# Inputs laid out transposed outside the program, layer-norm folds moved from VectorE to TensorE, x loaded on two queues

## Chip, cores and metric

The kernel runs on one core of a Trainium2 chip. The metric is the device time of one execution in microseconds (us). TensorE is called PE, VectorE DVE, ScalarE ACT, GpSimd POOL and SyncE SP; PEld is TensorE's loading of weights. One program holds five instruction streams that meet at semaphores.

## What is computed

x has 32 batches of 256 tokens with 128 channels, fp32. Two layers follow one another, each with a residual and a layer norm behind it.

```python
# layer 1: attention with one head, its q, k, v batch-normed over all tokens
Wm_attn = W_attn + (lora_attn_A @ lora_attn_B).reshape(W_attn.shape)
xa = einsum('btc,dc->btd', x, Wm_attn)
xa = (xa - mean) * rsqrt(var + 1e-5) * bn_gamma + bn_beta     # mean, var over batches and tokens
q, k, v = split(xa, 3)
y = softmax(causal(q @ k.T / sqrt(128))) @ v @ W_proj.T @ Wm_proj.T
x = layernorm(x + y)
# layer 2: the best 2 of 8 experts for each token
logits = ln(x, router_ln_scale, router_ln_bias) @ router_w.T + router_b
gates = top 2 of softmax(logits), normed to sum 1
expert e: gelu(ln(x, ls[e], lb[e]) @ w1[e].T + b1[e]) @ w2[e].T + b2[e]
x = layernorm(x + sum over e of gates * expert)
```

## The kernel before

**Prologue.** SP issues the loads of x in 16 chunks of four row tiles, then w1 and w2 (8 loads each), the broadcast of b2 and two fills of padding. ACT issues the small matrices, six small parameters, and, once chunk 11 is there, `b1c` and the broadcasts `ls_bc` and `ld_bc` (expert scale and shift to all partitions, 512 KB each, L849 and L852). PE adds up the Gram matrix of x (L650), because the batch norm's mean and variance of q, k and v follow from it. Between chunks PE and DVE fold the low-rank terms into the weights in four rounds (`fold_round`). Behind the last chunk DVE makes `cov` (L1052), PE the products `wmT` by `cov` (L661), DVE the variances (from L1060), POOL the root (L525), DVE the scaled weights, PE the matrix M for q and k (L667) and the value matrix (L670), and DVE copies M to `MT` (L1091). Between `cov` and the products DVE, in its order, waits for `ls_bc` and `ld_bc` and subtracts them (L1054). In the gaps PE transposes chunks of x into `xT` (`transpose_chunk`, L627), and ACT copies them out of PSUM (`copy_chunk`).

**Attention.** It is written as 34 unrolled steps (`attend_step` on PE, ACT and DVE), a pipeline over the batches: in step k PE makes z for batch k+1 (`make_z`, L691), its values (L696 is the constant part from `cv3`, L705 the product with `wvvT`), scores (L714 to L716), the transposes of the probabilities (L752), and the output of batch k-1 (L763 to L765). DVE takes the maxima (L1142), adds the output to x (L1149), chooses two experts for batch k-3, and writes for batch k-4 the rows at which its tokens go into the experts' queues (`pos_i`, L1196). POOL scatters the rows of a batch by four indirect DMAs (L538), for batches 0 to 19 while attention runs. Steps 3 to 6 also transpose the last four chunks of x, steps 7 to 22 the sixteen weight blocks (`transpose_weights`, L642), which ACT copies in the step behind. DVE folds expert scale, shift and first bias into w1 in three parts per expert (`fold_expert`), part by part in steps 1 to 21. `cv3`, the constant of the values as three bf16 parts, is made by three splits on DVE (L1099 to L1105) ahead of the steps.

**Experts.** 142 tiles of 128 queued rows pass through two products per tile (L803 and L813), POOL scatters the results, and DVE, POOL and ACT combine them and apply the last layer norm.

Of the kernel before, what the change touches and what calls it, by code (L numbers as in the profile page):

```python
# [28 lines left out]
BF16 = mybir.dt.bfloat16  # L29
# [59 lines left out]
def build(nc, x, w_attn, w_proj, la_a, la_b, lp_a, lp_b, gamma, beta, r_ls, r_lb, r_w, r_b,  # L89
          e_ls, e_lb, w1, b1, w2, b2, out):  # L90
    NB, T, C = x.shape
    E, H, _ = w1.shape
    R = la_a.shape[1]
# [29 lines left out]
    with ExitStack() as ctx:  # L123
# [17 lines left out]
        def carver(region):  # L141
# [31 lines left out]
        s_const = sem("s_const")  # L173
        s_mat, s_par, s_go = sem("s_mat"), sem("s_par"), sem("s_go")
        N_MAT, N_PARAM = 6, 6
# [8 lines left out]
        s_one, s_tr, s_ev, s_gram = sem("s_one"), sem("s_tr"), sem("s_ev"), sem("s_gram")  # L184
# [3 lines left out]
        wa = sb("wa", [P, 3, P])  # L188
        wp = sb("wp", [P, P])
        aA, aB = sb("aA", [P, R]), sb("aB", [R, 3 * P])  # L190
        pA, pB = sb("pA", [P, R]), sb("pB", [R, P])
        gb = sb("gb", [P, 2, 3])
        rls, rlb = sb("rls", [P, 1]), sb("rlb", [P, 1])
        rwT, rb = sb("rwT", [P, E]), sb("rb", [1, E])
        aAT, pAT = sb("aAT", [R, P]), sb("pAT", [R, P])
        wm = sb("wm", [P, 3, P])
# [28 lines left out]
        w_rows = sb("w_rows", [P, 2 * E * H])  # L225
        w2n = w_rows[:, 0:E * H].rearrange("p (e h) -> p e h", e=E)
        w1n = w_rows[:, E * H:2 * E * H].rearrange("p (e k d) -> p e k d", e=E, k=HC)
        EARLY_X = 12


        FOLD_STEP, X_STEP = 1, 3
        W_STEP = X_STEP + NCH - EARLY_X
        W1_FIRST = 2
        W_ORDER = [("w1", e) for e in range(W1_FIRST)] + [("w2", e) for e in range(E)] + [
            ("w1", e) for e in range(W1_FIRST, E)]

        def chunk_bank(c):
            return (0, 1, 6)[c % 3] if c < 9 else (1, 6, 1)[c - 9] if c < EARLY_X else 6

        def chunk_after(c):  # L240

            return max([n + 1 for n in range(c) if chunk_bank(n) == chunk_bank(c)], default=0)

        b1c = sb("b1c", [P, E * HC])
        ls_bc, ld_bc = sb("ls_bc", [P, E * P]), sb("ld_bc", [P, E * P])
        w1s = sb("w1s", [P, HC, P])
        w1k = sb("w1k", [P, HC])
        s_w1 = [sem(f"s_w1_{e}") for e in range(E)]
        s_w2, s_ls, s_w1p, s_wt, s_wc = [sem(n) for n in ("s_w2", "s_ls", "s_w1p", "s_wt", "s_wc")]
# [127 lines left out]
        def _(sp):  # L377

            def load_w1(e):
                sp.dma_start(w1n[:, e], w1[e].rearrange("(p k) d -> p k d", k=HC)).then_inc(s_w1[e], 16)  # L380

# [86 lines left out]
        def _(pool):  # L468
            pg = Progress(pool, s_pool)

# [7 lines left out]
            pg.did(pool.memset(zeros[:], 0.0))  # L478
            pg.did(pool.memset(inv_c[:], 1.0 / C))
# [6 lines left out]
            for g in range(2):  # L486
# [22 lines left out]
                                      fill=MASKED, base=0, channel_multiplier=1))  # L509
            pg.did(pool.affine_select(out=before[:], in_=ones_h[:], pattern=[[1, P]], compare_op=ALU.is_gt,  # L510
# [82 lines left out]
        def _(pe):  # L593
            mm, tr = pe.matmul, pe.transpose
            pe.wait_ge(s_one, 1)
            gram = bank[7][:, 0:P + 1]

            def fold_round(r):
                wait(pe, s_fold_dve, r)
                if r == 0:  # L600
                    pe.wait_ge(s_const, 1)
                    pe.wait_ge(s_mat, 16 * N_MAT)
                    tr(bank[5][0:R, 0:P], aA[:], ident[:])
                    last = tr(bank[5][0:R, P:2 * P], pA[:], ident[:])
                elif r == 1:
                    mm(bank[3][:, 0:3 * P], aAT[:], aB[:], start=True, stop=True)
                    mm(bank[2][:, 0:P], wp[:], ident[:], start=True, stop=False)
                    last = mm(bank[2][:, 0:P], pB[:], pAT[:], start=False, stop=True)
                elif r == 2:
                    for a in range(3):  # L610
                        tr(bank[4][:, a * P:(a + 1) * P], wm[:, a, :], ident[:])
                    mm(bank[2][:, P:2 * P], wp[:], wpmT[:], start=True, stop=True)
                    last = mm(bank[2][:, 2 * P:3 * P], wpmT[:], wp[:], start=True, stop=True)
                else:
                    mm(bank[2][:, 3 * P:3 * P + E], rls_bc[:], rwT[:], start=True, stop=True)
                    mm(bank[2][:, 3 * P + E:3 * P + 2 * E], rlb_bc[:], rwT[:], start=True, stop=False)
# [803 lines left out]
```

## Time and the profile before

| what | value |
|---|---|
| time of the kernel, median of 3 runs | 638.56 us (638.44 to 638.88) |
| the profiled execution: time, and span of its instructions | 633.27 us, 631.5 us |
| granted PE clock, mean over the span | 0.873 of full |
| PE busy, PEld busy | 476.5 us, 448.1 us |
| DVE, ACT, POOL busy | 287.1, 364.6, 301.9 us |
| DMA | 53.70 MB, mean 85 GB/s |

The profile is of one execution. Its own time is 0.8% below the median of the others, so a sum made in its microseconds is laid on that execution first. The busy time of an engine says what it did and not whether anyone waited for it; the chain of waits, followed back from the last instruction, says that. "Granted clock" 1.00 is 2.4 GHz for PE, 0.50 is 1.2 GHz. A release that no semaphore event on the core explains is printed as "remote" or "another core or an unknown queue".

### The profile page before, as it was taken

The numbers are of one execution on the slowest core, as the hardware profiler recorded it, in microseconds if no ns is written. First come the engines' busy times: TensorE is split into PE (matmuls) and PEld (weight loads), VectorE is DVE, ScalarE is ACT, GpSimd is POOL, SyncE is SP. The second block draws the span as 40 slices with busy tenths as digits, with TensorE's granted clock in tenths as the row PEclk, the third lists the DMA queues.
The fourth block names the chain that finished last, engine by engine and source line by source line (L and its number), as shares of the span: only waits on it lengthen the run. The fifth ranks groups of instructions, "written<-read, shape, count | busy, mean of one in ns | idle before, by whom it ended". The sixth has DMA issues, their size and how long they took to land.

```text
span 631.5 us, 15137 instructions
## 1 busy us (share of the span) xinstructions
PE 476.5 (75%) x3652; PEld 448.1 (71%) x3652; DVE 287.1 (45%) x1617; ACT 364.6 (58%) x934; POOL 301.9 (48%) x361
## 2 busy tenths in 40 slices
PE   7969566585756959777778887778899999999300
PEld 6868455575655859777767876777899999999300
DVE  0178454655545964222222221212333588783393
ACT  0338354553643866544454554445677788998483
POOL 4002655556552005445655444545344476675573
PEclk9979797897977979878889777788799999999755
DMA  9950111111112012222221221222122456543362
GB/s 227 358 147 14 44 44 40 35 40 44 39 44 62 2 32 69 59 60 78 74 66 56 57 56 54 58 61 60 53 65 80 139 155 168 168 121 115 91 195 72
DMA packets 66049, 53.70 MB, mean 85 GB/s; under 512 B 11986, under 2 KB 59218, under 8 KB 65970
## 3 DMA queue, kind: packets, MB, share of 16 engines
q1 hardware_dynamic: 53136, 33.27, 19.8%
q0 software_dynamic: 8640, 17.97, 8.7%
q10 hardware_dynamic: 4194, 1.53, 1.0%
q8 instruction: 34, 0.56, 0.4%
q14 instruction: 45, 0.37, 0.2%
HBM read 28.43 MB, written 24.31 MB: 84 GB/s over the span
## 4 chain that ended last, share of the span: by engine, by line
PE 64%; another core or an unknown queue 11%; issue 6%; ACT 6%; DVE 5%; DMA 5%; SPq 2%; ACTq 0%; POOL 0%; POOLq 0%; DVEq 0%
PE bank L803 24%; PE bank L813 22%; PE bank L796 3%; PE bank L705 3%; DMA ld_bc<-L_ffn_expert_ln_bias 2%; PE bank L691 2%; SPq L383 1%; PE bank L714 1%; PE bank L763 1%; PE bank L752 1%; DMA xT<-ybuf 1%; DMA x_all<-L_attn_x 1%; PE bank L765 1%; PE bank L764 1%
## 5 line engine op out<-in xcount | busy, mean ns | idle before, releaser
L549 POOL DMA_INDIRECT ybuf<-xT,yrow x142 | 137.3, 967 | 183.5 <-DVE yrow L1278 134.9
L803 PE MATMUL bank<-xT 128*128 128x128 f32 x1136 | 167.9, 296 | 34.3 <-issue 20.0
L803 PEld LDWEIGHTS bank<-xT 128*128 128x128 f32 x1136 | 152.3, 209 | 36.8 <-issue 21.6
L813 PE MATMUL bank<-w2T,xT 128*128 x1136 | 164.9, 292 | 13.1 <-ACT xT L948 11.5
L538 POOL DMA_INDIRECT queue<-x_all,pos_i x128 | 123.1, 962 | 94.6 <-DVE pos_i L1196 56.3
L813 PEld LDWEIGHTS bank<-w2T,xT 128*128 128x128 f32 x1136 | 150.7, 206 | 17.2 <-issue 16.7
L1268 DVE TENSOR_TENSOR xT<-bank,b_bc 128x128 f32<-128x128 f32 x142 | 41.4, 292 | 221.5 <-PE bank L813 120.4
L835 ACT ACTIVATE xT<-w1T,zero_col 128x512 f32 x142 | 102.3, 721 | 31.2 <-issue 24.0
L948 ACT ACTIVATE xT<-bank 128x512 f32<-128x512 f32 x142 | 82.7, 583 | 23.8 <-PE bank L803 21.0
L835 ACT ACTIVATE xT<-bank,one_col 128x128 f32<-128x128 f32 x142 | 51.6, 364 | 76.0 <-remote 35.7
L1275 DVE TENSOR_SCALAR xT<-xT 128x128 f32<-128x128 f32 x142 | 49.4, 348 | 2.4 <-issue 1.5
L835 ACT ACTIVATE zT<-bank,u_z 128x256 f32<-128x256 f32 x32 | 15.1, 471 | 57.0 <-remote 43.5
L796 PE MATMUL bank<-ident,xT 128*128 128x128 f32 x142 | 41.4, 291 | 3.9 <-DVE xT L1275 2.4
L714 PE MATMUL bank<-xT,zT 128*128 128x128 f32 x64 | 15.3, 325 | 38.1 <-ACT zT L835 38.1
L714 PEld LDWEIGHTS bank<-xT,zT 128*128 128x128 f32 x64 | 10.9, 214 | 40.8 <-ACT zT L835 40.8
L953 ACT ACTIVATE x_all<-x_all,sh,r 128x128 f32<-128x128 f32 x64 | 27.9, 483 | 8.3 <-DVE sh L1336 6.7
L1149 DVE SCALAR_TENSOR_TENSOR x_all<-bank,rinv,x_all 128x136 f32<-128x136 f32 x64 | 20.0, 354 | 27.2 <-remote 22.2
L1319 DVE SCALAR_TENSOR_TENSOR x_all<-xT,gates,x_all 128x128 f32<-128x128 f32 x100 | 31.0, 351 | 2.7 <-DMA xT<-ybuf 2.5
L1278 DVE SCALAR_TENSOR_TENSOR yrow<-xT,tab_bc 128x1 int32<-128x1 f32 x142 | 30.6, 215 | 0.0
L835 ACT ACTIVATE xT<-bank,zero_col 128x512 f32<-128x512 f32 x16 | 10.3, 693 | 31.8 <-PE bank L627 31.8
L763 PE MATMUL bank<-vs,prT 128*128 128x136 f32 x64 | 17.0, 351 | 14.3 <-ACT prT L835 9.4
L796 PEld LDWEIGHTS bank<-ident,xT 128*128 128x128 f32 x142 | 21.2, 150 | 7.8 <-issue 7.2
(220 smaller groups left out, 750.5 us busy)
## 6 DMA issues: line engine op xcount, KB each, us to landing
xT<-queue SPq DMA_DIRECT2D x142, 66.0 KB
xT<-ybuf SPq DMA_DIRECT2D x32, 256.0 KB
x_all<-L_attn_x SPq DMA_DIRECT2D x16, 256.0 KB, 6.2
w_rows<-L_ffn_w SPq DMA_DIRECT2D x16, 256.0 KB, 8.8
out<-x_all SPq DMA_DIRECT2D x32, 128.0 KB
ybuf<-xT,yrow POOLq DMA_INDIRECT x142
queue<-x_all,pos_i POOLq DMA_INDIRECT x128
queue<-pad_rows SPq DMA_DIRECT2D x2, 528.0 KB, 13.7
```

Of the source, the lines that this page charges most:

```text
L538: pool.indirect_dma_start(out=queues[b >= NB0], out_offset=bass.IndirectOffsetOnAxis(pos_i[:, b, t, c:c + 1], 0), in_=x_all[:, b * TPB + t ...
L549: pool.indirect_dma_start(out=ybuf, out_offset=bass.IndirectOffsetOnAxis(yrow[:, q:q + 1], 0), in_=ysb[:, q, :], in_offset=None).then_inc( ...
L714: mm(sc[:, 0:P], zT[:, s, 0:P], x0, start=False, stop=False)
L796: tr(bank[q % 2][:, 0:P], xg[:, q % XR, 0:P], ident[:]).then_inc(s_gt, 1)
L803: last = mm(bank[2 + s][:, h * P:(h + 1) * P], w1c[:, (q - 1) % XR, h * P:(h + 1) * P], xgT[:, s, :], start=True, stop=True)
L813: last = mm(bank[4 + s][:, 0:P], hs[:, s, h, :], w2T[:, bass.ds(e, 1), h, :].rearrange("p a d -> p (a d)"), start=(h == 0), stop=(h == HC ...
L835: return act.activation(out_, in_, ACT.Identity, bias=bias)
L948: act.activation(hs[:, s].rearrange("p h t -> p (h t)"), bank[2 + s][:], ACT.Gelu).then_inc(s_hs, 1)
L1268: v.tensor_tensor(ysb[:, q, :], bank[4 + q % 2][:, 0:P], b2_bc[:, bass.ds(e * P, P)], ALU.add).then_inc(s_ys, 1)
L1275: v.tensor_scalar(row, row, xg[:, q % XR, MEAN - DATA:MEAN - DATA + 1], xg[:, q % XR, ROOT - DATA:ROOT - DATA + 1], ALU.subtract, ALU.mult ...
L1278: v.scalar_tensor_tensor(out=yrow[:, q:q + 1], in0=xg[:, q % XR, FIRST - DATA:FIRST - DATA + 1], scalar=tab_bc[:, bass.ds(k, 1)], in1=xg[: ...
L1319: yield v.scalar_tensor_tensor(out=row, in0=yb[:, n % U, t, k, :], scalar=gates[:, n * TPB + t, 1 - k:2 - k], in1=row, op0=ALU.mult, op1=A ...
```

## The change

`kernel()` hands the program other arrays: x once more as `x_t` (columns of x as rows, so `xT` is loaded), w1 and w2 transposed, all matrices with 128 rows side by side in `wide`, those with 64 rows in `low`, and b1 as three copies of its eight rows in `b1_rows`. So PE's transposes of x, of w1 and w2 and of the low-rank factors go, with ACT's copies; four fold rounds become two. The folds into w1 move to PE: `fold_l[e]` is a diagonal of the expert's scale with the centred shift added to each column (eight ACT instructions), one fp32 product over 512 columns applies it, and a bf16 product adds the first bias, split in three bf16 parts on DVE. Three experts are folded ahead of attention, five in steps 0 to 4. x's even chunks are issued by SP, the odd ones by ACT behind the small matrices. PE begins with seven products of zeros. Two of the three splits of `cv3` move behind DVE's step 0.

```diff
-            for c in range(NCH):
+            for c in range(0, NCH, 2):
                 load_chunk(c)
+            load_columns(0)
             for e in range(E):
-                load_w1(e)
+                sp.dma_start(w1r[:, e], w1_t[:, e]).then_inc(s_w1[e], 16)
+                if e == E - 2:
+                    load_columns(1)
+            for c in range(2, NB // XT_B):
+                load_columns(c)
             for e in range(E):
-                sp.dma_start(w2n[:, e, :], w2[e]).then_inc(s_w2, 16)
+                sp.dma_start(w2T[:, e], w2_t[:, e]).then_inc(s_w2, 16)
...
+            pe.wait_ge(s_warm, 1)
+            for n in range(N_WARM):
+                mm(bank[6][:, 0:P], warm[:], warm[:], start=True, stop=True)
...
-            ROUND_AFTER_CHUNK = {4: 0, 6: 1, 9: 2, 12: 3}
+            ROUND_AFTER_CHUNK = {4: 0, 8: 1}
+
+            def fold_w1(e):
+
+                pe.wait_ge(s_w1[e], 16)
+                if e == 0:
+                    pe.wait_ge(s_fl, 1)
+                    pe.wait_ge(s_b1s, 1)
+                wait(pe, s_wc, e if e > W1_FIRST else e - W1_FIRST + 1)
+                mm(fold_bank(e)[:], fold_l[:, e, :], w1r[:, e], start=True, stop=False)
+                mm(fold_bank(e)[:], pick_b[:, e, :], b1s[:], start=False, stop=True).then_inc(s_wt, 1)
...
-            for c in range(2):
-                transpose_chunk(c)
             pe.wait_ge(s_cov, 1)
-            mm(bank[2][:, 3 * P + 2 * E:3 * P + 3 * E], wp2[:], wvvT[:, 0:E], start=True, stop=True)
...
+            mm(bank[2][:, 3 * P + 2 * E:3 * P + 3 * E], wp2[:], wvvT[:, 0:E], start=True, stop=True).then_inc(s_wr, 1)
+            for e in range(W1_FIRST):
+                fold_w1(e)
             pe.wait_ge(s_qk, 1)
...
             def make_z(b):
+                if b % XT_B == 0:
+                    pe.wait_ge(s_xt[b // XT_B], 16)
...
-                if X_STEP <= k < W_STEP:
-                    transpose_chunk(EARLY_X + k - X_STEP)
-                elif W_STEP <= k < W_STEP + 2 * E:
-                    transpose_weights(k - W_STEP)
+                if k + W1_FIRST < E:
+                    fold_w1(k + W1_FIRST)
...
+            act.dma_start(low_s[:], low).then_inc(s_small, 16)
+            act.dma_start(wide_s[:], wide).then_inc(s_small, 16)
+            act.dma_start(rb[:], r_b.unsqueeze(0)).then_inc(s_small, 16)
...
+            for c in range(1, NCH, 2):
+                act.dma_start(x_all[:, c * CH:(c + 1) * CH, DATA:DATA + P], x_chunks[c]).then_inc(s_x[c], 16)
+                if c == 3:
+                    act.dma_start(b1f[:], b1_rows).then_inc(s_b1f, 16)
             act.wait_ge(s_const, 1)
-
...
+            act.wait_ge(s_dl, 1)
+            for e in range(E):
+                last = act.activation(fold_l[:, e, :], ident[:], ACT.Identity, bias=dl[:, e:e + 1],
+                                      scale=lsT[:, e:e + 1])
...
-                if X_STEP < k <= W_STEP:
-                    copy_chunk(EARLY_X + k - 1 - X_STEP)
-                elif W_STEP < k <= W_STEP + 2 * E:
-                    copy_weights(k - 1 - W_STEP)
+                if 0 < k <= E - W1_FIRST:
+                    copy_w1(k - 1 + W1_FIRST)
...
-            v.wait_ge(s_ls, 48)
-            op(v.tensor_tensor(ld_bc[:], ld_bc[:], ls_bc[:], ALU.subtract))
-            op(v.tensor_scalar(b1c[:], b1c[:], 1.0 / C, None, ALU.mult))
...
-            fold_expert(0, 0)
...
-            v.sem_inc(s_cv, 1)
-            fold_expert(0, 1)
-            fold_expert(0, 2)
+
+            split_constant(0)
...
-                if 0 <= k - FOLD_STEP < 3 * (E - 1):
-                    fold_expert(1 + (k - FOLD_STEP) // 3, (k - FOLD_STEP) % 3)
+                if known == 0:
+                    for n in range(1, 3):
+                        split_constant(n)
+                    v.sem_inc(s_cv, 1)
```

## Rows read from the trace of the kernel before

**Rows 1.** The page, the chain that ended last: share of the span by engine.

```profile
PE 64%; another core or an unknown queue 11%; issue 6%; ACT 6%; DVE 5%; DMA 5%; SPq 2%; ACTq 0%; POOL 0%; POOLq 0%; DVEq 0%
```

**Rows 2.** Timeline, prologue: start us, length us, engine, line, out<-in, [idle before <-releaser].

```profile
25.36 0.29 DVE L1052 TENSOR_SCALAR cov<-bank 128x129 f32<-128x129 f32 x1 [1.92 <-PE bank L650]
...
26.17 0.92 PE L661 MATMUL bank<-cov,wmT 128*128 128x129 f32 x6
...
37.19 0.28 DVE L1091 COPY MT<-bank 128x128 f32<-128x128 f32 x1
...
38.77 0.23 DVE L1099 CAST cvp<-cv 128x136 bf16<-128x136 f32 x1
...
40.60 0.22 DVE L1101 COPY cv<-cvp 1x272 bf16<-1x272 bf16 x1
...
42.21 0.29 PE L696 MATMUL bank<-cv,ones_b 128*128 128x288 bf16 x1
```

**Rows 3.** Chain of waits, prologue: start us, length us, what.

```profile
31.42 1.23 DVE ld_bc L1054
32.74 0.19 DVE scr L1060
...
36.06 0.80 PE bank L667 x2
...
38.19 1.71 PE bank L627 x8
```

**Rows 4.** Chain of waits, attention steps.

```profile
51.56 0.43 PE bank L691 x2
...
54.62 0.44 PE bank L627 x4
...
105.59 0.68 ACT w2T L835
```

**Rows 5.** Timeline of POOL: scatters, with POOL's idle time before one in brackets.

```profile
57.98 1.20 POOL L538 DMA_INDIRECT queue<-x_all,pos_i  x1 [17.52 <-DVE pos_i L1196]
...
85.31 0.96 POOL L538 DMA_INDIRECT queue<-x_all,pos_i  x1 [4.05 <-DVE pos_i L1196]
...
94.15 0.96 POOL L538 DMA_INDIRECT queue<-x_all,pos_i  x1 [0.31 <-issue]
...
103.70 0.95 POOL L538 DMA_INDIRECT queue<-x_all,pos_i  x1 [0.81 <-issue]
...
107.48 0.96 POOL L538 DMA_INDIRECT queue<-x_all,pos_i  x1 [0.30 <-issue]
...
112.54 0.96 POOL L538 DMA_INDIRECT queue<-x_all,pos_i  x1 [4.10 <-DVE pos_i L1196]
```

**Rows 6.** Waits of ACT, 43 to 228 us: total us, times, longest us.

```profile
ACT zT L835 <- remote: 43.5, 10, 6.8
```

**Rows 7.** Timeline of ACT: copies of z, with the idle time before.

```profile
96.72 0.47 ACT L835 ACTIVATE zT<-bank,u_z 128x256 f32<-128x256 f32 x1 [6.81 <-remote]
...
109.69 0.47 ACT L835 ACTIVATE zT<-bank,u_z 128x256 f32<-128x256 f32 x1 [1.92 <-remote]
```

**Rows 8.** Timeline of DVE: positions of a batch, and the next maxima.

```profile
87.83 0.18 DVE L1196 TENSOR_REDUCE pos_i<-ohr 128x4 int32<-128x32 f32 x1
...
89.58 0.29 DVE L1142 TENSOR_REDUCE nmax<-bank 128x1 f32<-128x128 f32 x1 [0.76 <-remote]
```

**Rows 9.** Timeline of PE in the Gram sums, and landing of the chunks of x.

```profile
18.66 2.84 PE L650 MATMUL bank<-x_all 128*128 128x129 f32 x24
...
DMA to landing us min/median/max: 3.1/6.2/7.7
```

**Rows 10.** Windows, prologue: busy us and instructions by engine, PEclk, DMA share, GB/s.

```profile
8.00:10.00 2.00, 2.00 (x12) 2.00 (x12) 0.00 (x0) 0.00 (x0) 0.00 (x0) 1.00 1.18 292
...
24.00:26.00 2.00, 2.00 (x20) 2.00 (x20) 0.29 (x1) 0.14 (x1) 0.00 (x0) 1.00 1.04 412
...
38.00:40.00 2.00, 2.00 (x11) 1.94 (x10) 1.61 (x7) 0.76 (x2) 0.00 (x0) 0.50 0.36 76
```

More of the change, by code:

```diff
@@ L183, in build, with taker, take @@
         s_x = [sem(f"s_x{c}") for c in range(NCH)]
-        s_one, s_tr, s_ev, s_gram = sem("s_one"), sem("s_tr"), sem("s_ev"), sem("s_gram")
+        XT_B = 4
+        s_xt = [sem(f"s_xt{c}") for c in range(NB // XT_B)]
+        s_one, s_gram, s_warm = sem("s_one"), sem("s_gram"), sem("s_warm")
         x_chunks = x.rearrange("b t c -> (b t) c").rearrange("(n j p) c -> n p j c", j=CH, p=P)
[L188 to L196, printed above, removed]
+        wide_s, low_s = sb("wide_s", wide.shape), sb("low_s", low.shape)
+        def taker(tile):
+            at = [0]
+            def take(n):
+                at[0] += n
+                return tile[:, at[0] - n:at[0]]
+            return take
+        take = taker(wide_s)
+        waT, wp, wpT, rwT, lsT, ldT = take(3 * P), take(P), take(P), take(E), take(E), take(E)
+        gb = take(6).rearrange("p (n a) -> p n a", n=2)
+        rls, rlb = take(1), take(1)
+        take = taker(low_s)
+        aB, aAT, pB, pAT = take(3 * P), take(P), take(P), take(P)
+        rb = sb("rb", [1, E])
         wmT = sb("wmT", [P, 3 * P])
@@ L222, in build, with fold_bank @@
         r_bias = sb("r_bias", [P, E])
[L225 to L247, printed above, removed]
+        w1r = sb("w1r", [P, E, H])
+        dl = sb("dl", [P, E])
+        fold_l = sb("fold_l", [P, E, P])
+        b1f = sb("b1f", [P, H])
+        b1p = sb("b1p", [P, H], BF16)
+        b1s = sb("b1s", [P, H], BF16)
+        own = sb("own", [P, E])
+        warm = sb("warm", [P, P])
+        pick_b = sb("pick_b", [P, E, P], BF16)
+        W1_FIRST = 3
+        def fold_bank(e):
+            return bank[(6, 4, 5)[e] if e < W1_FIRST else 6]
         s_w1 = [sem(f"s_w1_{e}") for e in range(E)]
-        s_w2, s_ls, s_w1p, s_wt, s_wc = [sem(n) for n in ("s_w2", "s_ls", "s_w1p", "s_wt", "s_wc")]
+        s_w2, s_wt, s_wc, s_dl, s_fl, s_b1s = [sem(n) for n in ("s_w2", "s_wt", "s_wc", "s_dl", "s_fl", "s_b1s")]
         U = 4
@@ L469, in _ @@
             pg = Progress(pool, s_pool)
+            pool.memset(warm[:], 0.0).then_inc(s_warm, 1)
             pool.memset(x_all[:, :, FIRST:FIRST + 1], 1.0).then_inc(s_one, 1)
@@ L509, in _ @@
                                       fill=MASKED, base=0, channel_multiplier=1))
+            for n in range(3):
+                pg.did(pool.affine_select(out=own[:], in_=own[:], pattern=[[-1, E]], compare_op=ALU.not_equal,
+                                          fill=1.0 / C, base=-32 * n, channel_multiplier=1))
+                pg.settle()
             pg.did(pool.affine_select(out=before[:], in_=ones_h[:], pattern=[[1, P]], compare_op=ALU.is_gt,
@@ L868, in _, with copy_w1 @@
+            last.then_inc(s_fl, 1)
+            def copy_w1(e):
+                act.wait_ge(s_wt, e + 1)
+                cp(w1T[:, e, :], fold_bank(e)[:], bias=zero_col[:]).then_inc(s_wc, 1)
+            for e in range(W1_FIRST):
+                copy_w1(e)
             act.wait_ge(s_mt, 1)
@@ L1097, in _, with split_constant @@
             pg.settle()
-            for n in range(3):
+            def split_constant(n):
                 op(v.tensor_copy(cvp[:, n, :], cv[:]))
```

196 lines of the change are left out of this document (82 added, 114 removed).

## The prediction

> **What bounds the kernel now.** I read the page first, then the chain of waits in order of time, then the timeline where the chain enters the edited code. By engine the chain gives PE 64% of the span, but 11% goes to "another core or an unknown queue" [rows 1]: there is one core here, so these are waits whose release the profile cannot name. Most of PE's share is the experts' stage, whose program the diff leaves alone. The change acts before that: in the prologue up to the first MATMUL of L691 (z of batch 0), and in the attention steps.
>
> The prologue first. The Gram sums end and `cov` is made at 25.36 [rows 2], yet the chain runs through the load of `ld_bc` until 31.42, then through the 1.23 us subtraction of L1054, and only at 32.74 does DVE begin the variances [rows 3]. The three products it needs began at 26.17 and took 0.92 [rows 2]: done by 27.1. So 5.6 us are lost because DVE, in program order, waits for a parameter of the experts. From 36.06 the M product runs, `MT` is ready at 37.47 (37.19 plus 0.28 [rows 2]), but PE first does eight transposes of x, 1.71 us, and z can start only at 39.9 (38.19 plus 1.71) [rows 3].
>
> Then the attention steps. In the early ones PE is the limit: L691 comes at 51.56 and again at 55.06, just behind 0.44 us of transposes of x: a step of 3.50 us [rows 4]. From the first scatter at 57.98 [rows 5] this changes. The view of waits has ACT standing 43.5 us in ten waits before `zT`, released by nothing named [rows 6]. Laid beside POOL's rows they have a pattern. POOL issues its scatters in bursts of eight (two batches): one from 85.31 to 95.11, the next until 108.44 (starts of the last scatters plus 0.96) [rows 5]. ACT's waits end at 96.72 and 109.69 [rows 7], 1.6 and 1.25 us behind the ends of the bursts, and the others lie alike. Inside a burst the maxima of DVE, which need PE's scores, start at 89.58 after 0.76 us with no named release; this lateness appears just behind the second batch's positions, written at 87.83 [rows 8]. I cannot say why PE's signals come late there; I take from the rows only that two batches pass per burst and that the wait lasts until the burst is over.
>
> **The change, part by part.**
>
> *Expert broadcasts gone.* DVE no longer waits for `ld_bc`, nor does L1054: 32.74 becomes 27.1, so -5.6 us. The load is late by itself; next late is the product, at 27.1. L659 goes behind the products (-0.2, not counted).
>
> *The Gram sums end earlier.* PE's rounds between chunks fall from four to two and the warm-up runs before data arrives. 24 records, three chunks, take 2.84 us [rows 9], so 16 chunks are 15 us, and with about twenty records at the same 0.12 us (2.4) for the two rounds left PE could be done at 4+17.4=21.4. The loads decide against that. x moves at 292 GB/s in 512-byte pieces, with larger pieces beside it all loads make 412 [rows 10]. Odd chunks queue on ACT behind `low`, `wide` (0.54 MB) and with `b1f` (0.26 MB); SP meanwhile goes on to columns and w1. If both queues get equal shares, 5.8 MB have moved when the last odd chunk lands: 4.2/0.29 + 1.6/0.4 = 18.5 us, from 2 us on, plus some landing time (3.1 to 7.7 us from issue now [rows 9]): 21 to 23.5. I take `cov` at 23.0: -2.4, bounds 0 and -4.
>
> The Trainium skill (Trainium Kernel Development and Optimization, Key Constraints) says that DMAs issued from SP, ACT and POOL run on the same 16 engines and that several issuers save only issue time. By it the second queue gives nothing of its own, and the term would be -1.5, from PE's shorter rounds; the sum would be 0.9 us weaker.
>
> *Variance to z.* From 32.74 to 36.06 are 3.3 us of DVE and POOL that stay. PE now works beside them on `fold_w1(0..2)`: a fp32 product of 512 columns costs twice the 0.43 us of L691's 256 columns [rows 4], plus 0.2 to 0.3 for the bf16 one (L696, 288 columns, is 0.29 [rows 2]): 1.1 us each, 3.3 in all. They start when the projection ends and end with the constants: hidden, but with no slack; at the half clock that PE has in this stretch now (0.50 granted, which is 1.2 GHz [rows 10]) they would cost +3.3. Since PE stays busy from the Gram on I take 0 there and the M product at the full clock. From M's start to z go 39.9-36.06=3.8 us now; without 1.71 of transposes and with faster products 1.3: -2.5. The columns of batch 0 land long before (ninth on SP's queue). Sum at z(0): -5.6-2.4-2.5 = -10.5.
>
> *Split constants.* Two of the three splits move behind DVE's step 0, and L696 waits for them. Now 42.21-39.9=2.3 us lie from z to L696 [rows 2]. Then: these 2.3, DVE's two maxima behind them (0.7 as an estimate), and two splits at 0.7 each (the three run from 38.77 to 40.82 [rows 2]): 4.4. +2.1 (bounds 0, +2.5). Leaves -8.4.
>
> *w1 folds in steps 0 to 4.* PE, the limit there [rows 4], gets 5 x 1.1 = 5.5 us and loses the two transpose groups of steps 3 and 4, 0.9. The first steps have a little idle PE (0.4): +4.2, bounds +1 (hidden behind ACT and DVE) and +5.5. ACT's copies, 0.7 each, fit beside. DVE loses all fold work, none of it on the chain here. Sum at the first scatter: -8.4+4.2 = -4.2.
>
> *Steps 5 to 23.* Three transposes of x and sixteen of weights leave PE, and their copies ACT. The chain has such pieces at 0.44 on PE, twice that at half the clock, and 0.68 on ACT [rows 4]; per four steps it takes one PE piece at either clock and two of ACT: 2.7 us, 12 in all. But four steps take two bursts of POOL and two restarts: from 85.31 to 112.54, 27.2 us. If the wait lasts until the burst is over, shorter steps make longer waits. What can shrink is the hole inside a burst, where the fifth scatter waits for the second batch's positions: at 103.70 POOL had stood 0.81 us instead of 0.3, so 0.5 us in every second burst [rows 5]. Five of them: -2.5. Bounds 0 and -12 (beyond that: rival). The restart from 109.69 to 112.54 is DVE's chain to the positions, without folds in it, and stays.
>
> *No cost, and what covers it.* About 3.4 MB more are loaded; DMA is idle from 39 us on [rows 10], xT's groups serve four batches each (12 us) and take 1.4 us, w2 is needed by the experts' stage alone. If cover fails, z(4) waits for xT's second group behind seven w1 loads. POOL's three selects of `own` come before the constants are asked for. Steps after 23 and the experts' stage: 0.
>
> Sum: -4.2-2.5 = -6.7. The profiled execution took 633.27 with a span of 631.5, 0.8% under the median 638.56; on its scale 626.6. Taken from the median: 631.9.
>
> **Rivals.**
>
> *A. The waits go by work, not by bursts* (20%). The unnamed waits would come at PE's own pace, whatever POOL does; then the 12 us of removed work count in full: -4.2-12 = -16.2, 622.4. For it: the removed pieces stand on the chain. Against: every wait ends just behind a burst. The Trainium skill has a rule of this kind (Runtime: NRT & Kernel Launch, Instruction fetch mechanics): code comes in 16 KiB blocks of 256 instructions, and crossing a boundary is mostly hidden; if the blocks were the cause, waits would follow the count of instructions, and fewer transposes would also mean fewer waits.
>
> *B. Three batches per burst* (5%). Shorter steps slip a third batch in and POOL is never without work: four scatters in 5.05 us (an eighth of a burst of 10.1 is 1.26) against 6.8 now, 20 x 1.75 = -35, about 600. Against: lateness starts with the second batch's positions, however long the step.
>
> *C. Absorbed* (7%). Folds at half clock (+3.3), no earlier Gram (+2.4) and no gain in the bursts (+2.5) cancel it: 638.
>
> *D. Slower: odd chunks late on ACT's queue* (8%). SP queues 12 MB. If the engines serve it first, and ACT gets a quarter of some 300 GB/s, its 2.9 MB (eight chunks, parameters) land at 2+38=40 us: `cov` at 40.5, 15 us later than now instead of 2.4 earlier. From there: +15+2.4-6.7 = +10.7, 649. It decides when the last odd chunk lands after about 30 us. For it: no row shows the two queues in long competition. Against: the deciding time is 8 us behind my estimate of the landing, so a moderate preference for SP is not enough.
>
> **How the numbers follow.** My case, two batches per burst, has 60%: 631.9, its own range 627 to 636 (Gram 0 to -4, folds +1 to +5.5, bursts 0 to -4). 8 in 10 is held by it and most of A: 618 to 636.5; outside are B, D, most of C and the tails. A measurement of this kernel tells 0.2% (1.3 us) from nothing. Faster 0.87: my case, A, B and a little of C; same 0.05; slower 0.08.
>
> **What would show it.** Right: `cov` near 23, variances within 1.6 us of it, z(0) near 29, L696 of batch 0 near 33.7, first scatter near 53.8, bursts of eight with about 26.7 us per two bursts, ten waits that end 1.2 to 1.6 us behind them and are together longer than 43.5. Wrong if: the bursts change length or their period falls under 25 us (A, B); PE's clock in the folds is 0.50; chunk 15 lands after 25; steps 0 to 4 are no longer than now; or anything in the experts' stage changes its length by more than 2 us.

## The result, and the profile after

The changed kernel takes 642.72 us (median of 20 runs, 638.83 to 651.72) against 638.61 before (20 runs beside them, 632.07 to 642.80): ratio 1.0076, 95% interval 1.0049 to 1.0102. It is slower by 0.8%; 631.9 had been forecast, and the time lies outside the forecast range of 618 to 636.5. Ratios here leave out executions over 1.5% above the kernel's fastest, so they are not exactly the quotients of the medians. The profiled execution took 642.8 us with a span of 639.9, 8.4 more than the span before. The mean granted clock of TensorE is 0.873 in both.

The page after, the chain by engine (against [rows 1]): unnamed waits have grown from 11% to 17%, DMA stands at 5% as before.

```profile
PE 60%; another core or an unknown queue 17%; DMA 5%; ACT 5%; DVE 5%; issue 4%; ACTq 2%; POOL 0%; SPq 0%; POOLq 0%; DVEq 0%
```

The chain of waits after, prologue (start us, length us, what). In [rows 3] it ran through parameters; now one transfer of x is 20.93 us of it, the last odd chunk.

```profile
12.87 20.93 DMA x_all<-x
33.84 2.10 PE bank L656 x8
...
38.20 1.91 PE bank L647 x2
```

The timeline of PE after, in the Gram sums (against [rows 9]), and of DVE where `cov` is made (against [rows 2]):

```profile
4.35 1.94 PE L656 MATMUL bank<-x_all 128*128 128x129 f32 x8
10.01 5.18 PE L656 MATMUL bank<-x_all 128*128 128x129 f32 x32 [3.72 <-DMA x_all<-x]
...
24.49 2.05 PE L656 MATMUL bank<-x_all 128*128 128x129 f32 x16 [1.08 <-DMA x_all<-x]
28.37 2.05 PE L656 MATMUL bank<-x_all 128*128 128x129 f32 x16 [1.82 <-DMA x_all<-x]
33.84 2.09 PE L656 MATMUL bank<-x_all 128*128 128x129 f32 x8 [3.42 <-DMA x_all<-x]
```

```profile
35.97 0.29 DVE L1041 TENSOR_SCALAR cov<-bank 128x129 f32<-128x129 f32 x1 [10.99 <-PE bank L656]
38.01 0.29 DVE L1045 CUSTOM_DVE_ANT_0 scr<-bank,wn 128x128 f32<-128x128 f32 x1 [1.75 <-PE bank L664]
```

PE is starved four times, 10.0 us in all, and `cov` comes at 35.97 where it was 25.36. The idle times before L656 grow towards the end (1.08, 1.82, 3.42): the chunks of one queue come ever later. The view of the source line that issues ACT's odd chunks says which queue:

```profile
L845 ACTq DMA_DIRECT2D x_all<-x x8: 399/1437/3217, 2.6 to 12.9; - x8
...
DMA to landing us min/median/max: 7.4/12.4/20.9
```

Windows after, the columns as in [rows 10]: the engines of DMA are full and move almost as much as before (379 GB/s in 24:26, where it was 412, and 394 in 34:36), so x is late for its share of them, not for their speed. PE has the half clock, 0.50 granted, from 34 to 40.

```profile
8.00:10.00 2.00, 0.00 (x0) 0.00 (x0) 0.93 (x3) 0.00 (x0) 0.24 (x3) 0.86 1.21 290
...
24.00:26.00 2.00, 1.51 (x13) 1.51 (x14) 0.94 (x2) 0.00 (x0) 0.00 (x0) 1.00 1.05 379
...
34.00:36.00 2.00, 1.93 (x8) 1.63 (x8) 0.03 (x1) 0.00 (x0) 0.00 (x0) 0.50 1.03 394
38.00:40.00 2.00, 2.00 (x3) 0.78 (x5) 1.19 (x10) 0.00 (x0) 0.72 (x1) 0.50 1.06 388
```

The attention steps. The timeline of POOL after, first scatters of bursts (against [rows 5]), and the waits from 45 to 235 us (against [rows 6]):

```profile
69.25 1.21 POOL L556 DMA_INDIRECT queue<-x_all,pos_i  x1 [21.29 <-DVE pos_i L1182]
...
83.75 0.96 POOL L556 DMA_INDIRECT queue<-x_all,pos_i  x1 [4.44 <-DVE pos_i L1182]
...
96.73 0.96 POOL L556 DMA_INDIRECT queue<-x_all,pos_i  x1 [3.12 <-DVE pos_i L1182]
...
111.22 0.96 POOL L556 DMA_INDIRECT queue<-x_all,pos_i  x1 [4.68 <-DVE pos_i L1182]
```

```profile
ACT zT L837 <- remote: 49.6, 10, 7.0
DVE nmax L1128 <- remote: 44.8, 9, 7.1
```

The timeline of ACT after, the copies of z behind the ends of the two bursts that POOL's idle times give (93.61 and 106.54; against [rows 7]):

```profile
93.82 0.47 ACT L837 ACTIVATE zT<-bank,u_z 128x256 f32<-128x256 f32 x1 [5.27 <-remote]
...
108.31 0.47 ACT L837 ACTIVATE zT<-bank,u_z 128x256 f32<-128x256 f32 x1 [3.81 <-remote]
```

Bursts are still of eight scatters: two of them go from 83.75 to 111.22, 27.5 us, where it was 27.2 from 85.31 to 112.54 [rows 5]. The ten waits are longer together, as forecast, but they no longer end 1.2 to 1.6 us behind the bursts: it is 0.2 us for four of them and 1.5 to 1.8 for six (before, over all ten, 1.1 to 1.7).

What is late in such a wait can be seen in the timeline of PE before, beside the copy of z at 96.72 [rows 7]:

```profile
89.16 0.60 PE L691 MATMUL bank<-xT,MT 128*128 128x256 f32 x2
...
97.24 0.80 PE L714 MATMUL bank<-xT,zT 128*128 128x128 f32 x2 [6.20 <-ACT zT L835]
```

By PE's records z is finished at 89.76, 7.0 us before ACT copies it, and then PE itself stands for 6.2 us. So PE had done the product, and the signal of it came late.

The first scatter is 11.3 us later than before, the copy `zT` of batch 0 3.3 us later (44.20 against 40.91).

### The profile page after: what moved, and what is told of

Read it like the earlier page. It is cut to its first block, busy times and chain, and to the rows that moved or that the text cites. A ratio compares the mean times of both kernels' runs of the same rounds, so it can differ in the third digit from the quotient of the medians.

```text
span 639.9 us, 14860 instructions
## 1 busy us (share of the span) xinstructions
PE 473.9 (74%) x3556; PEld 441.7 (69%) x3559; DVE 269.3 (42%) x1542; ACT 356.3 (56%) x918; POOL 303.2 (47%) x364
## 4 chain that ended last, share of the span: by engine, by line
PE 60%; another core or an unknown queue 17%; DMA 5%; ACT 5%; DVE 5%; issue 4%; ACTq 2%; POOL 0%; SPq 0%; POOLq 0%; DVEq 0%
PE bank L805 23%; PE bank L815 19%; DMA x_all<-x 3%; PE bank L798 3%; PE bank L709 2%; PE bank L695 2%; PE bank L766 2%; DMA xT<-ybuf 2%; PE bank L755 2%; ACTq L845 1%; PE bank L647 1%; PE bank L718 1%; PE bank L768 1%; PE bank L767 1%
## 5 line engine op out<-in xcount | busy, mean ns | idle before, releaser
L815 PE MATMUL bank<-w2T,xT 128*128 x1136 | 161.6, 288 | 7.6 <-ACT xT L938 5.8
L815 PEld LDWEIGHTS bank<-w2T,xT 128*128 128x128 f32 x1136 | 148.5, 204 | 10.4 <-issue 10.1
L1263 DVE TENSOR_SCALAR xT<-xT 128x128 f32<-128x128 f32 x142 | 48.1, 339 | 3.8 <-DMA xT<-queue 3.4
L1128 DVE TENSOR_REDUCE nmax<-bank 128x1 f32<-128x128 f32 x32 | 9.2, 288 | 57.5 <-remote 44.8
L766 PE MATMUL bank<-vs,prT 128*128 128x136 f32 x64 | 18.4, 375 | 13.8 <-issue 9.2
L656 PE MATMUL bank<-x_all 128*128 128x129 f32 x128 | 19.1, 312 | 10.0 <-DMA x_all<-x 10.0
## 6 DMA issues: line engine op xcount, KB each, us to landing
w1r<-w_t SPq DMA_DIRECT2D x8, 256.0 KB, 11.8
```

The source lines that it names most:

```text
L766: mm(bank[5][:, 0:VW], prT[:, s, 0, :], v0, start=True, stop=True)
L815: last = mm(bank[4 + s][:, 0:P], hs[:, s, h, :], w2T[:, bass.ds(e, 1), h, :].rearrange("p a d -> p (a d)"), start=(h == 0), stop=(h == HC ...
L1263: v.tensor_scalar(row, row, xg[:, q % XR, MEAN - DATA:MEAN - DATA + 1], xg[:, q % XR, ROOT - DATA:ROOT - DATA + 1], ALU.subtract, ALU.mult ...
```

## Experiments

Ratios are to the kernel before on the same chip, with 95% intervals. Where times inside an execution are compared, each is from one trace. In the thirteen traces with x on one queue `cov` came at 23.96 to 27.16, so differences of `cov` under some 3 us between two traces say nothing. e1 to e4 ran on one chip, e5 to e8 with h0 and h1 on a second, all labels with f on a third, all with g on a fourth. Most edits start from a version called "one queue" here (e1): the changed kernel with all 16 chunks of x on SP again.

**Undoing the split of x (e1), making SP wait (e2), and small pieces on SP (e3).**

```diff
-            for c in range(0, NCH, 2):
+            for c in range(NCH):
...
-            for c in range(1, NCH, 2):
-                act.dma_start(x_all[:, c * CH:(c + 1) * CH, DATA:DATA + P], x_chunks[c]).then_inc(s_x[c], 16)
-                if c == 3:
-                    act.dma_start(b1f[:], b1_rows).then_inc(s_b1f, 16)
+            act.dma_start(b1f[:], b1_rows).then_inc(s_b1f, 16)
```

> The changed kernel, with all 16 chunks of x issued by SP before its columns and weights; ACT issues only the small matrices and b1. Theory T (the two queues take turns packet by packet, so ACT's 512-byte pieces of x fall behind SP's 2 and 4 KB pieces): chunk 15 lands near 20 to 22 us, cov is made near 23 to 24.5 in place of 35.97, and the time falls by 9 to 12 us against the changed kernel, to about 632 to 634. Rival R (PE or the sheer number of bytes makes the Gram sums late): cov stays after 30 and the time within 4 us of the changed kernel.

Measured 628.25 us, ratio 0.9919 [0.9874, 0.9964]. `cov` comes at 24.15, `zT` of batch 0 at 30.80, the first scatter at 53.22. SP's chunks land 7.6 us after issue at the latest:

```profile
DMA to landing us min/median/max: 3.7/6.0/7.6
```

In e2 the split stays as in the changed kernel, and SP waits for the last chunk before it issues the columns and the weights:

```diff
+            sp.wait_ge(s_x[NCH - 1], 16)
```

> The changed kernel with x still on two queues; SP waits until chunk 15, ACT's last, is there before it issues columns and weights. Theory T: nothing with large pieces stands beside the odd chunks, chunk 15 lands near 20 to 21, cov near 22; the first columns and w1 then land later (24 to 28), so the first weight fold starts some 2 us late: time 6 to 11 us below the changed kernel. Rival R: cov hardly moves, and the delayed loads make it slower than the changed kernel.

Measured 634.06 us, ratio 1.0011 [0.9978, 1.0043]; `cov` at 28.72, where near 22 was expected, and a gain of some 4 us against the changed kernel's 1.0076, less than the 6 to 11 expected.

In e3 the loads of SP are cut up:

```diff
-                sp.dma_start(xT[:, here], x_t[:, here]).then_inc(s_xt[c], 16)
+                sp.dma_start(xT[:, here].rearrange("p (n t) -> p n t", t=P),
+                             x_t[c * n:(c + 1) * n].rearrange("n p t -> p n t")).then_inc(s_xt[c], 16)
```

and the same for w1 and w2: x's columns and the weights laid out in blocks, so that each contiguous piece is 512 bytes like x's own, the same bytes in all (e3).

> The changed kernel with the same bytes and the same order of issue, but the host lays x_t, w1_t and w2_t so that SP's loads of them move in pieces of 512 bytes. Theory T: with pieces of one size both queues get equal bytes, chunk 15 lands near 22 to 24, cov near 24 to 25, although the total rate falls from 390 to about 290 GB/s; the time falls by 6 to 11 us. Rival R (bytes and rate): a lower rate makes everything later, cov at 36 or after it, and the kernel slower.

Measured 632.59 us, ratio 0.9978 [0.9945, 1.0011]: 6 us better than the changed kernel, as expected, though `cov` had been expected at 24 to 25. The timeline of PE and DVE:

```profile
10.20 5.91 PE L660 MATMUL bank<-x_all 128*128 128x129 f32 x32 [4.61 <-DMA x_all<-x]
...
28.84 0.29 DVE L1045 TENSOR_SCALAR cov<-bank 128x129 f32<-128x129 f32 x1 [2.95 <-PE bank L660]
```

Smaller pieces on SP bring `cov` as far forward, 7.1 us, as taking SP's later transfers away altogether (28.84 and 28.72). PE then waits once, for chunk 1, behind `low` and `wide` on ACT's queue. The view of the DMA queues in a stretch of 2 us gives the records and MB of each queue; q1 carries SP's loads, q10 ACT's. For the changed kernel, 18 to 20 us:

```profile
q1 hardware_dynamic: 312, 0.57, 79.7%
q10 hardware_dynamic: 316, 0.15, 28.1%
```

The same view for other stretches (records, MB):

```
kernel, us       SP's queue    ACT's queue
after 12 to 14   595, 0.29     595, 0.30
after 22 to 24   300, 0.57     302, 0.15
after 28 to 30   184, 0.68     184, 0.09
after 30 to 32   188, 0.70     161, 0.08
e3    16 to 18   583, 0.30     581, 0.29
```

While both have work, the queues get nearly the same number of records, whatever their size (between 30 and 32 us ACT's last chunk runs out). As long as both send 512 bytes, that is the same rate. Once SP is at pieces of 2 KB and more, ACT's 512-byte pieces get 0.15 MB in 2 us (75 GB/s), then 0.09, then 0.08.

The Trainium skill states the rule (DMA: Bandwidth & Descriptors, Queues, rings and completion order): each engine takes turns between the queues that have work, packet by packet. The trace agrees in the equal counts; how many records make up one turn it does not show. The same page (Issuing engines are not separate DMA queues) says that issuing on several engines only saves the time to issue; here ACT's issues took 1.4 us each in the median (above, 1437 ns), SP's 0.5, and the second queue cost 11.8 us of `cov` (35.97 against 24.15).

The trace of the kernel before had shown this already. Its row of 24 to 26 us, 412 GB/s [rows 10], is the sum of two queues, SP's weights in 2 KB pieces and ACT's broadcasts in 4 KB pieces:

```profile
q10 hardware_dynamic: 169, 0.52, 65.2%
q1 hardware_dynamic: 165, 0.30, 38.9%
```

Equal records and unequal bytes, before anything was changed; no x was among them.

**Chunk 1 on SP as well (g3, e3 with this on top), and the changed kernel beside it (g0).**

```diff
-            for c in range(0, NCH, 2):
+            for c in (0, 1, *range(2, NCH, 2)):
...
-            for c in range(1, NCH, 2):
+            for c in range(3, NCH, 2):
```

> Columns and weights in pieces of 512 bytes as before, and chunk 1 of x also taken from ACT's queue and put second on SP's. With small pieces alone cov came at 28.8 and not at 24 to 25; PE there stood 4.6 us before the second chunk, which ACT had issued behind low and wide. If that is the rest of the delay, PE's hole between the first two chunks falls from 4.6 to under 1.5 us and cov comes at 24.5 to 26; the time 2 to 4 us below small pieces alone (ratio 0.988 to 0.995). If PE only meets the same wait one odd chunk later, cov stays at 28 or more.

> The changed kernel itself, unedited, on the chip of the three beside it, so that its ratio stands beside theirs. Expected ratio to the kernel before 1.005 to 1.012 if the chip has the unnamed waits.

g3: ratio 0.9948 [0.9913, 0.9984]; g0: 1.0161 [1.0104, 1.0218]. This is a chip on which the kernel before takes 485.95 us; its traces have none of the unnamed waits (below), and g0's expectation was for a chip that has them. `cov` is at 36.07 in g0, as after; in g3 the timeline of DVE has

```profile
25.30 0.29 DVE L1045 TENSOR_SCALAR cov<-bank 128x129 f32<-128x129 f32 x1 [2.95 <-PE bank L660]
```

PE's hole of 4.61 us before chunk 1 is gone (three waits of 0.46 to 1.18 us are left). So of the 11.8 us 7.1 go with the sizes (35.97 to 28.84) and about 3.5 with chunk 1 (to 25.30); the 1.2 left to 24.15 are within the differences of traces with one queue. g3 shows what comes next: its first batch's positions are ready at 54.85, but POOL scatters at 58.38, because before its first scatter it waits for SP's fill of the padding rows, which in small pieces lands only at 57.07.

**The split alone, in the kernel before (e4).** The odd chunks go to ACT, behind its parameters.

```diff
-            for c in range(NCH):
+            for c in range(0, NCH, 2):
...
+                for c in range(1, NCH, 2):
+                    act.dma_start(x_all[:, c * CH:(c + 1) * CH, DATA:DATA + P], x_chunks[c]).then_inc(s_x[c], 16)
```

> The kernel before, with one edit: the odd chunks of x are issued by ACT behind its twelve small loads. Theory T: the odd chunks stand beside SP's w1 and w2 in 2 KB pieces, the last lands near 28 to 32, cov moves from 25.4 to about 30 to 33, and since b1c and the two broadcasts are issued only when chunk 11 is there, they land near 36 to 40: slower by 5 to 12 us. Rival R: total bytes are the same as before, so no change beyond 2 us.

Measured 640.89 us, ratio 1.0116 [1.0085, 1.0146]. Timeline of PE and DVE:

```profile
20.12 6.53 PE L650 MATMUL bank<-x_all 128*128 128x129 f32 x32 [14.03 <-DMA x_all<-L_attn_x]
...
40.67 0.29 DVE L1054 TENSOR_SCALAR cov<-bank 128x129 f32<-128x129 f32 x1 [1.92 <-PE bank L650]
```

The time is as expected (5 to 12 us slower), `cov` is 8 us later than expected. The odd chunks stand behind the small strided parameters there: between 10 and 14 us ACT's queue moves 1795 records of 4 bytes, in turn with SP's (391 and 407 records between 12 and 14 us), and chunk 1 alone holds PE for 14.0 us. Moving the odd chunks to ACT's queue slows either kernel.

**The bursts.** All start from one queue; the edits in this order. Scatters apart (e5, f5): POOL waits for the last batch's scatters to land. Folds in bursts (e7, f7): those of w1 in steps 8 to 12, and ACT's copies with them. Sixteen more folds (e8, f8), done again for nothing, with their copies. Splits ahead (e6): all splits of the constants before the steps.

```diff
+                if b:
+                    pool.wait_ge(s_scat[(b - 1) % ROWS], SCAT * ((b - 1) // ROWS + 1))
```

```diff
-                if k + W1_FIRST < E:
-                    fold_w1(k + W1_FIRST)
+                if 0 <= k - 8 < E - W1_FIRST:
+                    fold_w1(k - 8 + W1_FIRST)
```

```diff
+        N_FOLD = E + 16
...
-                if k + W1_FIRST < E:
+                if k + W1_FIRST < N_FOLD:
```

```diff
-            split_constant(0)
+            for n in range(3):
+                split_constant(n)
+            v.sem_inc(s_cv, 1)
```

> x on one queue, and while attention runs POOL scatters a batch only when the scatters of the batch before have landed, so that two batches never stand back to back. Theory L (PE's signals come late only while POOL has a second batch queued behind the first, and until its burst is over): the unnamed waits of ACT and DVE in attention (some 45 us) mostly go, steps run at 3.3 us, attention ends 20 to 50 us earlier, though POOL now needs about 7 us a batch; the experts' stage starts when POOL is done, so the time falls by 5 to 25 us against x on one queue. Rival W (the waits come at PE's own pace, from its instructions): the waits stay, and POOL's extra pauses make it equal or slower.

> x on one queue, and all three splits of the value constant made ahead of the steps, as in the kernel before. By the term of the prediction L696's counterpart of batch 0 comes 2.3 to 2.6 us behind z instead of 4.3, so the first scatter comes about 2 us earlier. Theory L: that passes to the end, -1 to -2 us. Rival: the splits delay DVE's first maxima by as much and nothing changes, within 1 us.

> x on one queue, and the five w1 folds that stand in steps 0 to 4 moved to steps 8 to 12, where the scatters run. Theory L: PE waits there until a burst of scatters is over, and the folds' 5 x 1.07 us on PE and 5 x 0.7 us on ACT are hidden by that wait; steps 0 to 4 fall from 4.1 to 3.1 us, the first scatter comes 4 to 5 us earlier, and the time falls by 3 to 5 us. Rival W (the waits go by work): the 5 us only change their place and the time stays within 1.5 us.

> x on one queue, and every w1 fold done three times: sixteen more in steps 5 to 20, each 1.07 us of PE and 0.7 us of ACT, 17 us of PE in all, with the same results. Theory L: in the steps with scatters the work takes the place of waiting: slower by 0 to 5 us, and the unnamed waits shrink by 10 us or more. Rival W: slower by 12 to 20 us.

These four came to a chip on which the kernel before takes 486.48 us, with no unnamed wait in any trace: e5 1.0669 [1.0614, 1.0724], e6 0.9887 [0.9839, 0.9935], e7 0.9869 [0.9814, 0.9924], e8 1.0177 [1.0127, 1.0228]. So they say nothing of the waits beside bursts. Three were run once more, with one queue beside them:

> x on one queue, run again as the base for the three beside it: the kernel before took 633.7 us on the chip of the first four runs and 486.5 us on that of the next four, whose traces have no unnamed waits at all, so runs of different chips can't be compared. If this chip has the unnamed waits: ratio to the kernel before 0.988 to 0.996, as on the first. If it has none: without waits that take gains back, the 10 us won by z(0) less what the folds cost should be kept or, if POOL's scatters (5.05 us a batch) bound the start of the experts' stage, appear as the earlier first scatter, 4 to 6 us: ratio 0.987 to 0.992.

> x on one queue, POOL scattering a batch only when the batch before has landed. If the chip has the unnamed waits: theory L expects them gone in attention and the kernel 5 to 25 us faster than x on one queue; rival W equal or slower. If the chip has none: slower by some 37 us, as the trace of the first try shows (POOL at 7 us a batch is the bound).

> x on one queue, five folds moved from steps 0 to 4 to steps 8 to 12. With unnamed waits: theory L -3 to -5 us against x on one queue, rival W within 1.5 us. Without them: POOL's 5.05 us a batch is slower than the steps of 3.3 to 4.4 us, so folds beside the scatters are hidden by POOL and the first scatter comes 4 to 5 us earlier: -3 to -5 us as well.

> x on one queue, sixteen folds more in steps 5 to 20 (17 us of PE). With unnamed waits: theory L +0 to +5 us against x on one queue, rival W +12 to +20. Without them: steps of 4.4 us in place of 3.3 run until 160 us, behind POOL's last scatter of the first group, so PE becomes the bound: +10 to +16 us.

On this chip the kernel before takes 633.41 us and has the waits: f1 0.9951 [0.9920, 0.9981], f5 0.9573 [0.9492, 0.9653], f7 0.9874 [0.9829, 0.9920], f8 0.9950 [0.9907, 0.9992].

f8 against f1 is the test of what bounds the steps. What sixteen folds cost PE, the page's line of busy times shows on the chip without waits, of e8 here and of one queue (h0) below: 435.5 us busy against 418.2, 17.3 more.

```profile
PE 435.5 (89%) x3607; PEld 404.6 (82%) x3607; DVE 270.4 (55%) x1542; ACT 364.0 (74%) x934; POOL 303.0 (62%) x364
```

On the chip with waits they cost nothing within some 3 us, 0.9950 beside 0.9951, and the unnamed waits are shorter: 107.5 us between 45 and 225 us against 131.3 in f1 and 130.7 in e1. The work took the place of waiting, as theory L had it. On the chip without, the same edit costs 1.0177 - 0.9871 = 3.1%, 15 us of the 17. Where the waits are, PE's work in the steps is not what counts. f8 tests PE's time and not its count of instructions, of which the folds add few (3607 records against 3556).

f7 gains 0.8%, 4.9 us, on f1, as theory L had it (3 to 5); e7 gains nothing on one queue on its chip (0.9869 beside 0.9871), where as much was expected. The `cov` of e7's trace came 3.1 us later than h0's, and one trace doesn't say whether its other executions lost their gain by that.

f5 has POOL's timeline and waits (45 to 225 us):

```profile
90.35 0.96 POOL L556 DMA_INDIRECT queue<-x_all,pos_i  x1 [2.20 <-DMA queue<-x_all,pos_i]
...
97.24 0.96 POOL L556 DMA_INDIRECT queue<-x_all,pos_i  x1 [2.14 <-DMA queue<-x_all,pos_i]
...
104.13 0.96 POOL L556 DMA_INDIRECT queue<-x_all,pos_i  x1 [2.14 <-DMA queue<-x_all,pos_i]
```

```profile
POOL queue L556 <- DMA queue<-x_all,pos_i: 37.2, 17, 2.4
ACT x_all L839 <- remote: 21.0, 7, 4.0
DVE nmax L1127 <- remote: 16.2, 6, 3.1
...
ACT zT L839 <- remote: 3.5, 1, 3.5
```

With 2.2 us of rest between the batches' scatters, `zT` has 3.5 us of unnamed waits where f8 and f1 on the same chip have 27.7 each, all engines together 67.5 against 107.5 and 131.3 (f1's profiled execution took 636.61 us against its median of 629.46). That is half and not most of them, which theory L had expected. A batch passes every 6.9 us (13.7 per two), and the kernel is 3.8% faster than f1. So the waits do depend on POOL's scatters standing back to back, and not on the amount of PE's work. PE's program is the same in f5 as in f1, so its count of instructions does not set them either. This speaks for the burst theory and against rival A; how POOL's scatters hold the signals up is not shown. Where there are no such waits the same rest is pure loss, 1.0669 to 0.9871 or 8% (e5 against h0 below).

**On the chips without waits (g1, g2, h0, h1).** g1 is e5 with e7; g2 is g1 with the scatters of the later batches, in the experts' stage, spread one by one. h1 is e6 with e7, beside one queue (h0).

> x on one queue, five folds in steps 8 to 12, and each batch of scatters only behind the landing of the last. With unnamed waits: the two gains (some 5 and 24 us against x on one queue) are for one thing, time lost beside POOL's bursts, so they add only in part: POOL at 6.9 us a batch from the first scatter is the bound, which comes 3 to 4 us earlier: ratio to the kernel before 0.948 to 0.957. Without them: about 1.06.

> As the kernel with folds moved and scatters apart, and in the experts' stage POOL issues the four scatters of a batch one by one behind four results, not four in a row. If the unnamed waits of that stage (some 80 us of DVE's idle time) also come from POOL working back to back, they shrink and the time falls by 5 to 30 us. Rival: POOL is behind anyway for those tiles (1.26 us for a result and 1.26 for a scatter against some 2 us a tile), its run of back-to-back work only stretches, and the time stays or rises by up to 10 us.

> x on one queue, as the base beside the kernel with folds moved and splits ahead. On a chip with the unnamed waits 0.992 to 0.995 of the kernel before; on one without them 0.990 to 0.995, since the first scatter comes 5 us earlier and POOL at 5.05 us a batch passes that on.

> x on one queue, five folds in steps 8 to 12, all three splits ahead of the steps. Against x on one queue on the same chip: -3 to -5 us for the folds and -1 to -2 for the splits, both by an earlier first scatter: ratio to the kernel before 0.980 to 0.989 on either kind of chip.

g1 1.0560 [1.0509, 1.0612], g2 1.0643 [1.0578, 1.0708]: both came to a chip without the waits, so whether g2 helps where they are stays open. h0 0.9871 [0.9822, 0.9920], h1 0.9753 [0.9705, 0.9801]. g1 is where it was expected on such a chip (about 1.06), g2 4 us slower than g1, as its rival had it, but within the intervals; h0 and h1 are better than expected (0.990 to 0.995 and 0.980 to 0.989). h1 beats both kernels: the one before by 2.5%, and the changed one by some 4%, taken over the chips (g0 had 1.0161 on the other chip without waits). Its first scatter is at 48.85, h0's at 54.49, each in the timeline of POOL:

```profile
48.85 1.20 POOL L556 DMA_INDIRECT queue<-x_all,pos_i  x1 [1.07 <-issue]
```

```profile
54.49 1.20 POOL L556 DMA_INDIRECT queue<-x_all,pos_i  x1 [6.93 <-DVE pos_i L1179]
```

The page of h0, busy times, to set beside e8's line above:

```profile
PE 418.2 (88%) x3556; PEld 396.9 (83%) x3559; DVE 270.5 (57%) x1542; ACT 355.1 (74%) x918; POOL 302.3 (63%) x364
```

h1's two edits alone (e6, e7) had shown nothing beyond one queue within their intervals of 0.5%. Together they give 1.2%, some 5.7 us. Counted from `cov`, one trace of each shows how it divides: the first batch's positions (`pos_i`) come 2.8 us earlier than in h0 with the splits ahead (e6), 3.5 us with the folds moved (e7), 6.1 with both (h1). In h1 they are ready at 47.32, and the first scatter comes only at 48.85: POOL waits there for the padding rows, as in g3, which bounds this gain.

```profile
47.53 0.24 POOL L546 IOTA pad_rows<- 128x16 f32 x1 [20.10 <-DMA queue<-pad_rows]
```

On the chips with waits h1 was not run.

## Why the prediction was wrong

**The step that failed is "The Gram sums end earlier".** It took equal shares of bytes for the two queues and had the last odd chunk land at 21 to 23.5 us, `cov` at 23.0. It landed at 33.80 (12.87 plus 20.93), `cov` at 35.97: the term is +10.6, not -2.4, 13.0 us off. The row I had used, 412 GB/s [rows 10], I had misread: there are no pieces of x in that stretch, and it is two queues at 165 and 169 records with 0.30 and 0.52 MB. Read by queue, it shows that records are shared and not bytes, and it stood in the trace before the forecast was made. What the runs showed in its place: queues share by records, so that large pieces on one starve small ones on the other (7.1 us, e3, and the equal counts), and the first odd chunk waits behind `low` and `wide` (about 3.5 us, g3). This is rival D's event, to which I gave 8%, at a lower price. D decided at a landing after 30 us; 33.8 is beyond it. D's quarter for ACT was right in size for 18 to 24 us (0.15 of 0.72 MB in 18 to 20 is 21%) and too pessimistic for the time before SP turned to large pieces, when it had half.

With that step taken back (e1) the kernel is 0.8% faster, about 5.1 us, where the sum had 6.7; with the failed term at its e1 value, -1.2, the sum would have been 5.5. That they lie so close is in part luck. By e1's trace the lead of 4.8 us at the first scatter has shrunk to 1.6 at the first expert scatter (235.83 against 237.39), and the other 3.7 us lie in the experts' stage, for which the sum had nothing. f1, the same kernel on another chip, is ahead by 0.5%, 3.1 us.

The other steps, each as after and e1 measured it against the trace of before:

- *Expert broadcasts, -5.6:* from `cov` to the first variance are 1.32 us in e1 (24.15 to 25.47) and 2.04 after, against 7.38: -6.1 and -5.3. Right.
- *Variance to z, -2.5:* with the step before it, `cov` to `zT` is 6.65 us in e1 against 15.55: -8.9, forecast -8.1. After it is 8.23, -7.3, as the folds ran at the half clock. That was one of my signs of being wrong, and it followed from the first: PE stood waiting for x and had 0.50 from 34 to 40. The fp32 product of the first fold took 1.91 us where that of the third took 0.86. Up to z(0) e1 gained 10.1, forecast 10.5; the changed kernel lost 3.3.
- *Splits +2.1, folds +4.2:* from `zT` of batch 0 to the first scatter +5.4 in e1 (22.42 against 17.07), forecast +6.3; after it was +8.0, again with a half clock in the first two steps. One by one, against h0: splits 2.8 (e6), forecast 2.1; folds 3.5 (e7), forecast 4.2. Steps with a fold take 4.14 us, before 3.50.
- *Steps 5 to 23, -2.5:* this step failed too, by 4.4 us after and 5.7 in e1. That bursts and not work set the pace held; that the closed hole would shorten them did not. Two bursts take 27.2 to 27.5 us, before 27.2 to 27.3; 12 us of work less on the chain gave nothing, as 17 us more took nothing (f8). The hole inside every second burst is gone, 0.5 us as forecast, but POOL's restarts behind the bursts grew by 0.7: 3.12 and 4.68 against 2.97 and 4.10 in [rows 5]'s sequence. From first scatter to first expert scatter: +1.9 after (181.4 against 179.4), +3.2 in e1.
- *Experts' stage, 0:* from its first scatter to the end 389.3 us, before 394.1: -4.8, more than the 2 us I had allowed. In the ten traces of the chips with waits, e4 with before's own program among them, it is 389.3 to 394.1, and one kernel alone gave 390.4 (e1) and 393.4 (f1). So I count this as scatter of one execution; what makes it was not tried.

The parts add up: +10.6 - 7.3 + 8.0 + 1.9 - 4.8 = +8.4, the difference of the spans. The medians have half of it, 4.1, since the execution before that was profiled was 0.8% under its median.

Rival A, waits that go by PE's work, is refuted (f8, f5); nor does the changed kernel bear it out, whose unnamed waits are 125.6 us against 93.8 with less work in the steps. B occurred in part: e1 and f1 have bursts of twelve scatters, once and twice, with no time gained. C and its price were not at issue.

## What to carry to other kernels

Before moving a load to a second queue, compare the sizes of the contiguous pieces on both: the queues got equal numbers of records, so the queue with small pieces got 512 bytes for every 2 to 4 KB of the other, and what stands on the critical path must not be the one with small pieces. A row that sums all queues hides this; read it queue by queue. A load that must be early belongs first on the queue that has nothing ahead of it; issuing it beside bulk transfers shares the engines, and holding those back (e2) or cutting them up (e3) is second best. Where an engine's work hides inside a wait of another origin, add work for nothing before you count on removing it: f8 says in one run whether the stage is bound by it.

## What the runs showed of the hardware

- The kernel before took 639 us in the runs beside the result, 633 to 634 on two chips and 486 to 487 us on two others. The traces of the chips with 486 to 487 have no wait without a named release between 45 and 225 us; elsewhere it is 93.8 us in the kernel before, 125.6 after and 67.5 (f5) to 131.3 (f1) in its variants (all engines' rows summed). Of the 148.7 us between the spans of e1 and h0, the same kernel, 70.0 lie between the first scatter and the first expert scatter and 79.9 in the experts' stage, whose waits no run looked into where they occur. An experiment on such waits must run where they are.
- On the chips with waits, signals of PE come late while POOL issues indirect DMAs back to back (7.0 us behind PE's record of z at 89.16), and ACT gets them 0.2 to 1.8 us behind the end of the burst; 2.2 us of rest after each four scatters halves the waits (f5). Why, and why only on some chips, was not found.
- Between the two DMA queues records were served nearly one for one, 312 to 316 in 2 us, at some 1.8 KB on one side and 0.5 KB on the other on average, and 165 to 169 in the kernel before, at 1.8 and 3.1 KB.
